# Taking the warm-up matmuls off TensorE in an attention and feed-forward kernel

## Chip, cores and metric

The kernel runs on one core of a Trainium2 chip. The metric is the device time of one execution in microseconds (us). The kernel before takes 144.61 us (median of 3 runs, 144.1 to 144.9).

## What is computed

The reference is a transformer block in float32 over x of 8 batches x 256 tokens x 128 features: single-head attention on the layer-normalised input, layer norm and residual, then a four-layer feed-forward with ternary weights and per-output scales, layer norm and residual.

```python
def attn(x, W_qkv):                       # W_qkv: 384 x 128
    q, k, v = split(einsum('bnd,ed->bne', x, W_qkv))
    a = softmax(einsum('bnd,bmd->bnm', q * 128 ** -0.5, k))
    return einsum('bnm,bmd->bnd', a, v)

def ffn(x):                               # 128 -> 512 -> 512 -> 512 -> 128
    h = silu((x @ w1.T) * s1) * ((x @ w2.T) * s2)
    h = gelu((h @ h1.T) * sh1)
    h = gelu((h @ h2.T) * sh2)
    return (h @ w3.T) * s3

x = x + layernorm(attn(layernorm(x), W_qkv))
x = x + layernorm(ffn(layernorm(x)))
```

## The kernel before

The 16 tiles of 128 tokens go through the kernel in five blocks of 2, 4, 4, 4 and 2 tiles. Each engine has one instruction stream, written out by hand; an instruction that needs another engine's result waits on a semaphore at its place in the stream, and all that stands behind it on its engine waits too. So the order of calls at the end of each engine's function is the schedule.

The stages of block b, by the names of the functions on TensorE: x_transposes(b) transposes the normalised input (matmuls against the identity `ident`, line 941); g_projection(b) multiplies it with the product of the query and key weights, which qk_product computes once from `wa_raw` (line 1121); v_projection(b) gives the values; scores(b, g) the scores of batch g of the block; probs_transposes(b, g) transposes the exponentials (line 992); attend(b, g) multiplies them with the values; attention_transposes(b) turns the result back (line 1017); x2_transposes(b) transposes the layer-normed sum (line 1024); up(b, o) computes both up-projections of hidden slice o (lines 1049, 1052); begin and end of A1, A2 and A3 are the layers h1, h2 and w3 (lines 1085, 1091); y_transposes(b) turns the block's output back (line 1112). Products of float32 data are made of high and low parts of type f32r: in the attention part each product is three matmuls (high x high, high x low, low x high), all issued in `product` (line 916).

Between the stages the other engines work. ScalarE copies the high part of each PSUM tile (xT_high, gT_high, v_high, pT_high, x2T_high, all through line 281), splits the weights (w12_high, h1_high, line 371), sums the low halves of the weights (low_sum, line 393) and computes exp, silu and gelu. VectorE writes the low parts (line 578), the row maxima neg_max (line 623), the layer-norm statistics and the normalised rows xn (line 595). GpSimd sets constants at the start (lines 226 to 231, `ident` among them) and computes the reciprocal roots (line 236). SyncE issues the loads in one order: x of block 0, the attention weights, x of block 1, w12, the scales, h1, x of block 2, h2, and so on.

keep_warm(bank, n) issues n matmuls of 128 x 128 weights with 256 columns of bf16, all read from the tile `warm` of zeros that GpSimd sets in its first own instruction (line 226). Their results land in a PSUM bank that holds nothing needed then, and nobody reads them. TensorE waits for `warm` before its first group. The groups and their places are in the order at the end of the TensorE function: 10 at the very start, 12 after qk_product, 8 after x_transposes(0), 1 ahead of g_projection(1), 3 ahead of scores(1, 0), 2 ahead of probs_transposes(1, 0) and 12 ahead of probs_transposes(1, 1); 48 in all.

Of the kernel before, what the change touches and what calls it, by code (L numbers as in the profile page):

```python
# [7 lines left out]
P = 128  # L8
# [17 lines left out]
def width(b):  # L26
    return SIZES[b] * P


def tiles(b):  # L30
    return slice(T0[b], T0[b + 1])
# [10 lines left out]
def sandwich_kernel(nc, x, w_attn, w12, h1, h2, w3, scales, out):  # L42
# [9 lines left out]
    with ctx:  # L52
        def sb(name, shape, dt=f32):
            return ctx.enter_context(nc.sbuf_tensor(name, shape, dt))

        def bank(name):
            return ctx.enter_context(nc.psum_tensor(name, [P, 512], f32))

        def sem(name):
            return ctx.enter_context(nc.semaphore(name))  # L60
# [13 lines left out]
        ident = sb("ident", [P, P])  # L74
        minus_half = sb("minus_half", [P, TB])
        ones = sb("ones", [P, 1])
        warm = sb("warm", [P, 512], mybir.dt.bfloat16)
        low_bits = sb("low_bits", [P, KT * HID])
        low_sums = sb("low_sums", [P, 4])
        flags = sb("flags", [1, 4])  # L80
# [36 lines left out]
        F = [bank(f"F{i}") for i in range(4)]  # L117
        A = [bank(f"A{i}") for i in range(4)]
# [26 lines left out]
        x_loaded = [sem(f"x_loaded{b}") for b in range(BLOCKS)]  # L145
        wa_loaded, w12_loaded, sc_loaded = sem("wa_loaded"), sem("w12_loaded"), sem("sc_loaded")
        h1_loaded, h2_loaded, w3_loaded = sem("h1_loaded"), sem("h2_loaded"), sem("w3_loaded")
        warm_ready = sem("warm_ready")
        zeroed, ident_ready = sem("zeroed"), sem("ident_ready")
        qk_summed, qk_copied, qk_split, qk_ready = sem("qk_summed"), sem("qk_copied"), sem("qk_split"), sem("qk_ready")  # L150
        wv_split, wv_ready = sem("wv_split"), sem("wv_ready")
# [39 lines left out]
        @block.sync  # L191
        def _(sp):
            def load_x(b):
                sp.dma_start(xs[:, tiles(b), :].rearrange("p (g j) d -> p g (j d)", j=2),
                             x_view[:, G0[b]:G0[b + 1], :]).then_inc(x_loaded[b], 16)

            def store(b):
                if b == LAST:
                    sp.wait_ge(last_ready, 1)
                else:  # L200
                    sp.wait_ge(out_ready, b + 1)
                sp.dma_start(out_view[:, G0[b]:G0[b + 1], :],
                             outs[:, tiles(b), :].rearrange("p (g j) d -> p g (j d)", j=2)).then_inc(out_stored, 16)

            load_x(0)
            sp.dma_start(wa_raw[:, :], w_attn).then_inc(wa_loaded, 16)
            load_x(1)
            sp.dma_start(w12_raw[:, :], w12).then_inc(w12_loaded, 16)
            sp.dma_start(sc[:, :], scales).then_inc(sc_loaded, 16)
            sp.dma_start(h1_raw[:, :, :], h1.rearrange("(k p) o -> p k o", p=P)).then_inc(h1_loaded, 16)  # L210
            load_x(2)
            sp.dma_start(h2_raw[:, :, :], h2.rearrange("(k p) o -> p k o", p=P)).then_inc(h2_loaded, 16)
            load_x(3)
            load_x(4)
            sp.dma_start(w3_raw[:, :], w3).then_inc(w3_loaded, 16)
            store(0)
            store(1)
            store(2)
            store(3)
            store(4)  # L220
            sp.wait_ge(out_stored, 16 * BLOCKS)


        @block.gpsimd
        def _(pool):
            nc.gpsimd.memset(warm[:, :], 0.0).then_inc(warm_ready, 1)  # L226
            nc.gpsimd.memset(ident[:, :], 0.0).then_inc(zeroed, 1)
            nc.gpsimd.memset(minus_half[:, :], -0.5).then_inc(zeroed, 1)
            nc.gpsimd.memset(ones[:, :], 1.0).then_inc(zeroed, 1)
            pool.wait_ge(zeroed, 3)  # L230
            nc.gpsimd.affine_select(out=ident[:, :], in_=ident[:, :], compare_op=ALU.not_equal, fill=1.0, base=0,
                                    pattern=[[-1, P]], channel_multiplier=1).then_inc(ident_ready, 1)

            def rsqrt(ln, b):
                pool.wait_ge(var_ready[ln], b + 1)
                nc.gpsimd.tensor_tensor(rstd[:, ln, tiles(b)], ve[:, ln, tiles(b)], minus_half[:, 0:SIZES[b]],  # L236
                                        ALU.pow).then_inc(rstd_ready[ln], 1)

            def lo_part(n, b, o):
                c = slice(0, width(b))  # L240
                pool.wait_ge(a_hi_ready[n], KT * b + o + 1)
                pool.wait_ge(a_full[n], KT * b + o + 1)
                nc.gpsimd.tensor_tensor(a_lo[n][:, o, c], act_full[:, o, c], a_hi[n][:, o, c].bitcast(f32),
                                        ALU.subtract).then_inc(a_lo_pool[n], 1)

            def last_add(b):
                pool.wait_ge(yn_ready, T0[b + 1])
                pool.wait_ge(x1_ready, b + 1)
                nc.gpsimd.tensor_tensor(outs[:, tiles(b), :], y_n[:, 0:SIZES[b], :], x1[:, tiles(b), :], ALU.add).then_inc(out_ready, 1)

            rsqrt(LN_X, 0)
            rsqrt(LN_X, 1)
            rsqrt(LN_X, 2)
            rsqrt(LN_O, 0)
            rsqrt(LN_X1, 0)
            rsqrt(LN_O, 1)
            rsqrt(LN_X1, 1)
            rsqrt(LN_X, 3)
            rsqrt(LN_X, 4)
            rsqrt(LN_Y, 0)  # L260
            rsqrt(LN_O, 2)
            rsqrt(LN_X1, 2)
            rsqrt(LN_Y, 1)
            rsqrt(LN_O, 3)
            last_add(0)
            last_add(1)
            rsqrt(LN_X1, 3)
            rsqrt(LN_Y, 2)
            rsqrt(LN_O, 4)
            last_add(2)  # L270
            rsqrt(LN_X1, 4)
            rsqrt(LN_Y, 3)
            last_add(3)
            rsqrt(LN_Y, 4)
# [636 lines left out]
        def _(pe):  # L911
# [18 lines left out]
            def read_flag(n):  # L930
                pe.wait_ge(flags_ready, (1, 1, 2, 2)[n])
                flag[n] = pe.value_load(flags[0:1, n:n + 1].bitcast(mybir.dt.int32))

            def x_transposes(b):
                if b > 1:
                    pe.wait_ge(gT_ready, b)
                    if SIZES[b - 1] == 4:
                        pe.wait_ge(pT_ready, G0[b])
                for t in range(SIZES[b]):
                    pe.wait_ge(xn_ready, T0[b] + t + 1)  # L940
                    last = nc.tensor.transpose(lane(b).xT_bank[:, t * P:(t + 1) * P], lane(b).xn[:, t, :], ident[:, :])
                last.then_inc(xT_in_psum, 1)

            def g_projection(b):
                c = slice(0, width(b))
                pe.wait_ge(xT_ready, b + 1)
                if b == 0:
                    pe.wait_ge(qk_ready, 1)
                product(lane(b).gT_bank[:, c], [(qk_hi[:, :], qk_lo[:, :], lane(b).xT[0][:, c], lane(b).xT[1][:, c])]).then_inc(gT_in_psum, 1)
# [16 lines left out]
            def scores(b, g):  # L966
                s = lane(b).s_bank[g]
                (x_hi, x_lo), (g_hi, g_lo) = lane(b).xT, lane(b).gT
                pe.wait_ge(gT_ready, b + 1)
                if b > 1 and g == 0:  # L970
                    pe.wait_ge(x2T_ready, b)
                if b > 1 and g == 1:
                    pe.wait_ge(oT_ready, b)
                keys = slice(g * SEQ, (g + 1) * SEQ)
                for j in range(2):
                    c = slice((2 * g + j) * P, (2 * g + j + 1) * P)
                    last = product(s[:, j * SEQ:(j + 1) * SEQ], [(g_hi[:, c], g_lo[:, c], x_hi[:, keys], x_lo[:, keys])])
                last.then_inc(scores_ready, 1)
# [133 lines left out]
                    last = nc.tensor.transpose(A[2][:, t * P:(t + 1) * P], yT[:, t * P:(t + 1) * P], ident[:, :])  # L1112
                last.then_inc(y_in_psum, 1)

            def keep_warm(bank, n):
                for _ in range(n):
                    nc.tensor.matmul(bank[:, 0:256], warm[:, 0:P], warm[:, 0:256], start=True, stop=True)  # L1117

            def qk_product():
                pe.wait_ge(wa_loaded, 16)  # L1120
                nc.tensor.matmul(F[3][:, 0:D], wa_raw[:, 0:D], wa_raw[:, D:2 * D], start=True, stop=True).then_inc(qk_summed, 1)

            pe.wait_ge(warm_ready, 1)
            keep_warm(A[0], 10)
            qk_product()
            pe.wait_ge(ident_ready, 1)
            keep_warm(A[0], 12)
            x_transposes(0)
            keep_warm(A[0], 8)
            g_projection(0)  # L1130
            x_transposes(1)
            v_projection(0)
            scores(0, 0)
            keep_warm(F[0], 1)
            g_projection(1)
            v_projection(1)
            probs_transposes(0, 0)
            keep_warm(F[3], 3)
            scores(1, 0)
            attend(0, 0)  # L1140
            scores(1, 1)
            attention_transposes(0)
            sum_flags(0)
            keep_warm(F[3], 2)
            probs_transposes(1, 0)
            read_flag(W12)
            read_flag(H1)
            keep_warm(F[3], 12)
            probs_transposes(1, 1)
            x2_transposes(0)  # L1150
            attend(1, 0)
# [136 lines left out]
```

## Time and profile before

| | |
|---|---|
| median of 3 runs | 144.61 us |
| the profiled execution | 144.72 us |
| its span, first to last instruction | 142.9 us |
| TensorE matmul busy | 127.7 us (89%), 749 matmuls |
| VectorE busy | 112.7 us (79%) |
| ScalarE busy | 113.3 us (79%) |
| GpSimd busy | 24.7 us (17%) |
| warm-up matmuls busy (30 into A, 18 into F) | 6.1 and 2.6 us |
| mean granted TensorE clock over the span | 0.991 |

The profiled execution is 1.8 us longer than its span. Busy time of TensorE is that of pipelined matmuls: the duration of one matmul contains its way through the array, so that the distance between two starts, not the duration, says how fast the engine takes them. PE is TensorE's matmuls, PEld its weight loads, ACT ScalarE, DVE VectorE, POOL GpSimd. A line such as L916 is the line of the kernel that issued the instruction; several stages share a helper's line, so they are told apart by their place in time and by their tiles. The tiles of block 0 borrow a part of act_full, a_hi and a_lo, so `act_full` or `a_hi` in an attention row of the first 20 us is block 0. The granted clock is 1.00 for TensorE at 2.4 GHz and 0.50 at 1.2 GHz.

### The profile page before, as it was taken

The numbers are of one execution on the slowest core, as the hardware profiler recorded it, in microseconds if no ns is written. First come the engines' busy times: TensorE is split into PE (matmuls) and PEld (weight loads), VectorE is DVE, ScalarE is ACT, GpSimd is POOL, SyncE is SP. The second block draws the span as 40 slices with busy tenths as digits, with TensorE's granted clock in tenths as the row PEclk, the third lists the DMA queues.
The fourth block names the chain that finished last, engine by engine and source line by source line (L and its number), as shares of the span: only waits on it lengthen the run. The fifth ranks groups of instructions, "written<-read, shape, count | busy, mean of one in ns | idle before, by whom it ended". The sixth has DMA issues, their size and how long they took to land.

```text
span 142.9 us, 2559 instructions
## 1 busy us (share of the span) xinstructions
PE 127.7 (89%) x749; PEld 106.7 (75%) x749; DVE 112.7 (79%) x362; ACT 113.3 (79%) x218; POOL 24.7 (17%) x33
## 2 busy tenths in 40 slices
PE   6987977999978999999999999999799999799930
PEld 3766855899975888888868888877578888589820
DVE  1766898999958998998889968958997597597553
ACT  3176998999999874949859996999964999968930
POOL 3400211002500000702000025510002052002301
PEclk9999999999999999999999999999999999999996
DMA  4999000000000000000000000120000002000021
GB/s 125 277 367 366 24 7 0 0 5 2 0 5 0 0 0 7 0 5 0 0 0 0 5 2 0 41 76 0 0 0 5 0 5 73 0 0 7 0 76 37
DMA packets 3857, 5.41 MB, mean 38 GB/s; under 512 B 384, under 2 KB 2560, under 8 KB 3840
## 3 DMA queue, kind: packets, MB, share of 16 engines
q1 hardware_dynamic: 3840, 5.19, 11.1%
q8 instruction: 10, 0.16, 0.4%
q14 instruction: 7, 0.06, 0.1%
HBM read 4.14 MB, written 1.05 MB: 36 GB/s over the span
## 4 chain that ended last, share of the span: by engine, by line
PE 53%; ACT 18%; issue 10%; DVE 8%; DMA 5%; POOL 2%; SPq 2%; POOLq 1%; DVEq 0%; ACTq 0%
PE F L1085 16%; PE F L1091 16%; PE A L916 8%; DMA h_raw<-h 5%; PE F L1049 4%; PE F L1052 3%; ACT a_hi L351 3%; ACT act_full L343 3%; ACT h_hi L371 2%; DVE act_full L666 2%; ACT silu L335 2%; DVE a_lo L578 1%; PE A L992 1%; DVE stats L582 1%; ACT probs L289 1%
## 5 line engine op out<-in xcount | busy, mean ns | idle before, releaser
L578 DVE TENSOR_TENSOR a_lo<-act_full,a_hi 128x512 fp32r<-128x512 f32 (+1 forms) x60 | 34.3, 595 | 6.6 <-ACT act_full L343 5.8
L236 POOL TENSOR_TENSOR rstd<-ve,minus_half 128x4 f32<-128x4 f32 (+1 forms) x20 | 18.9, 949 | 109.5 <-DVE ve L589 89.6
L1085 PE MATMUL F<-a_hi,h_hi 128*128 128x512 f32 (+1 forms) x160 | 37.4, 355 | 0.2 <-DVE act_full L666 0.2
L1091 PE MATMUL F<-a_lo,h_hi 128*128 128x512 f32 (+1 forms) x160 | 36.5, 350 | 0.0
L1091 PEld LDWEIGHTS F<-a_lo,h_hi 128*128 128x128 f32 x160 | 26.8, 189 | 4.2
L1085 PEld LDWEIGHTS F<-a_hi,h_hi 128*128 128x128 f32 x160 | 25.9, 189 | 4.0 <-DVE act_full L666 0.4
L351 ACT ACTIVATE a_hi<-F,sc 128x512 fp32r<-128x512 f32 (+1 forms) x40 | 24.2, 629 | 5.6 <-PE F L1091 5.4
L343 ACT ACTIVATE act_full<-F,sc 128x512 f32<-128x512 f32 (+1 forms) x40 | 24.3, 638 | 0.0
L666 DVE SCALAR_TENSOR_TENSOR act_full<-F,sc,silu 128x512 f32<-128x512 f32 (+1 forms) x20 | 12.5, 640 | 2.4 <-ACT silu L335 2.1
L335 ACT ACTIVATE silu<-F,sc 128x512 f32<-128x512 f32 (+1 forms) x20 | 11.5, 602 | 3.4 <-PE F L1052 3.3
L1049 PE MATMUL F<-x2T_hi,w_hi 128*128 128x512 f32 (+1 forms) x40 | 11.4, 367 | 1.7 <-DVE act_full L666 1.1
L1052 PE MATMUL F<-x2T_lo,w_hi 128*128 128x512 f32 (+1 forms) x40 | 10.9, 353 | 0.0
L1049 PEld LDWEIGHTS F<-x2T_hi,w_hi 128*128 128x128 f32 x40 | 6.3, 189 | 3.9 <-issue 2.3
L582 DVE BATCH_NORM_STATS2 stats<-A 128x6 f32<-128x128 f32 x30 | 6.8, 285 | 1.7 <-PE A L1112 1.5
L335 ACT ACT_TABLE_LOAD x6 | 7.7, 1283 | 0.1
L1052 PEld LDWEIGHTS F<-x2T_lo,w_hi 128*128 128x128 f32 x40 | 7.0, 189 | 1.1
L1117 PE MATMUL A<-warm 128*128 128x256 bf16 x30 | 6.1, 381 | 1.3 <-POOL warm L226 1.3
L585 DVE BATCH_NORM_AGGREGATE mv<-stats 128x2 f32<-128x6 f32 x64 | 6.5, 159 | 0.7
L1091 PE MATMUL A<-a_lo,w_hi 128*128 128x512 f32 (+1 forms) x20 | 5.8, 364 | 1.4 <-DVE a_lo L578 1.4
L674 DVE CAST a_hi<-act_full 128x512 fp32r<-128x512 f32 (+1 forms) x20 | 6.9, 367 | 0.1
L289 ACT ACTIVATE probs<-A,neg_max 128x256 f32<-128x256 f32 x14 | 6.5, 476 | 0.0
L351 ACT ACT_TABLE_LOAD x5 | 6.4, 1283 | 0.1
(137 smaller groups left out, 235.4 us busy)
## 6 DMA issues: line engine op xcount, KB each, us to landing
h_raw<-h SPq DMA_DIRECT2D x2, 1024.0 KB, 8.9
xs<-x SPq DMA_DIRECT2D x3, 256.0 KB, 7.9
out<-outs SPq DMA_DIRECT2D x3, 256.0 KB, 2.1
w_raw<-w SPq DMA_DIRECT2D x1, 512.0 KB, 4.9
xs<-x SPq DMA_DIRECT2D x2, 128.0 KB, 5.9
w_raw<-w SPq DMA_DIRECT2D x1, 256.0 KB, 9.2
out<-outs SPq DMA_DIRECT2D x2, 128.0 KB, 1.7
wa_raw<-w_attn SPq DMA_DIRECT2D x1, 192.0 KB, 2.4
```

The lines of the kernel that those rows point to most:

```text
L236: nc.gpsimd.tensor_tensor(rstd[:, ln, tiles(b)], ve[:, ln, tiles(b)], minus_half[:, 0:SIZES[b]], ALU.pow).then_inc(rstd_ready[ln], 1)
L335: nc.scalar.activation(silu1[:, o % 2, c], F[2 * (o % 2)][:, c], ACT.Silu, scale=sc[:, S_W1 + o:S_W1 + o + 1]).then_inc(silu_ready, 1)
L343: nc.scalar.activation(act_full[:, o, c], F[o][:, c], ACT.Gelu, scale=sc[:, s:s + 1]).then_inc(a_full[n], 1)
L351: nc.scalar.activation(a_hi[n][:, o, c], F[o][:, c], ACT.Gelu, scale=sc[:, s:s + 1]).then_inc(a_hi_ready[n], 1)
L578: nc.vector.tensor_tensor(dst, full, hi.bitcast(f32), ALU.subtract).then_inc(done, 1)
L582: last = nc.vector.bn_stats(stats[:, ln, T0[b] + t, :], tile(t))
L666: nc.vector.scalar_tensor_tensor(act_full[:, o, c], F[2 * (o % 2) + 1][:, c], sc[:, S_W2 + o:S_W2 + o + 1], silu1[:, o % 2, c], ALU.mult, ...
L916: last = nc.tensor.matmul(out, w, v, start=(n == 0 and m == 0), stop=(n == len(terms) - 1 and m == 2))
L1049: nc.tensor.matmul(bank, w_hi, x_hi, start=True, stop=False)
L1052: last = nc.tensor.matmul(bank, w_hi, x_lo, start=False, stop=True)
L1085: nc.tensor.matmul(out, terms[k][0], terms[k][2], start=(k == 0), stop=False)
L1091: last = [nc.tensor.matmul(out, terms[k][0], terms[k][3], start=False, stop=(k == KT - 1)) for out, terms in groups]
```

## The change

The seven calls of keep_warm, the function, the wait for `warm`, the memset on GpSimd, the semaphore and the tile are taken out. The order of all else on every engine stays.

```diff
-        warm = sb("warm", [P, 512], mybir.dt.bfloat16)
...
-        warm_ready = sem("warm_ready")
...
-            nc.gpsimd.memset(warm[:, :], 0.0).then_inc(warm_ready, 1)
...
-            def keep_warm(bank, n):
-                for _ in range(n):
-                    nc.tensor.matmul(bank[:, 0:256], warm[:, 0:P], warm[:, 0:256], start=True, stop=True)
-
...
-            pe.wait_ge(warm_ready, 1)
-            keep_warm(A[0], 10)
             qk_product()
             pe.wait_ge(ident_ready, 1)
-            keep_warm(A[0], 12)
             x_transposes(0)
-            keep_warm(A[0], 8)
             g_projection(0)
             x_transposes(1)
             v_projection(0)
             scores(0, 0)
-            keep_warm(F[0], 1)
             g_projection(1)
             v_projection(1)
             probs_transposes(0, 0)
-            keep_warm(F[3], 3)
             scores(1, 0)
             attend(0, 0)
             scores(1, 1)
             attention_transposes(0)
             sum_flags(0)
-            keep_warm(F[3], 2)
             probs_transposes(1, 0)
             read_flag(W12)
             read_flag(H1)
-            keep_warm(F[3], 12)
             probs_transposes(1, 1)
```

## Rows read from the trace of the kernel before

**Rows 1.** The page, part 4: the ended-last chain's shares of the span, by engine.

```profile
PE 53%; ACT 18%; issue 10%; DVE 8%; DMA 5%; POOL 2%; SPq 2%; POOLq 1%; DVEq 0%; ACTq 0%
```

**Rows 2.** That chain in order of time: start us, us, what.

```profile
12.70 2.25 PE A L916 x15
...
23.50 0.50 PE F L1024 x2
...
28.65 0.48 ACT silu L335
```

**Rows 3.** TensorE's timeline: start us, us (all matmuls of the row), line, tiles, count.

```profile
1.31 2.32 PE L1117 MATMUL A<-warm 128*128 128x256 bf16 x10 [1.31 <-POOL warm L226]
3.62 0.80 PE L1121 MATMUL F<-wa_raw 128*128 128x128 f32 x2
4.21 2.77 PE L1117 MATMUL A<-warm 128*128 128x256 bf16 x12
6.77 0.61 PE L941 MATMUL F<-ident,act_full 128*128 128x128 f32 x2
7.19 1.06 PE L1117 MATMUL A<-warm 128*128 128x256 bf16 x8
8.84 0.39 PE L916 MATMUL F<-a_hi,qk_hi 128*128 128x256 f32 x1 [0.59 <-DVE a_lo L578]
...
13.04 0.40 PE L916 MATMUL A<-xT_lo,qk_hi 128*128 128x512 f32 x1
13.27 0.39 PE L916 MATMUL A<-xT_hi,qk_lo 128*128 128x512 f32 x1
...
14.79 0.62 PE L992 MATMUL F<-ident,act_full 128*128 128x128 f32 x4
...
18.37 0.38 PE L1017 MATMUL F<-ident,act_full 128*128 128x128 f32 x2
...
19.21 0.65 PE L992 MATMUL A<-ident,probs 128*128 128x128 f32 x4
...
22.50 0.66 PE L992 MATMUL A<-ident,probs 128*128 128x128 f32 x4 [0.25 <-ACT probs L289]
...
24.38 0.35 PE L916 MATMUL A<-pT_hi,v_hi 128*128 128x256 f32 x1 [0.39 <-issue]
```

**Rows 4.** Timelines of ScalarE and VectorE in the same stretch.

```profile
7.96 0.37 ACT L281 ACTIVATE a_hi<-F 128x256 fp32r<-128x256 f32 x1
...
13.28 0.47 ACT L289 ACTIVATE act_full<-F,neg_max 128x256 f32<-128x256 f32 x1 [1.08 <-DVE neg_max L623]
...
15.45 0.60 ACT L281 ACTIVATE a_hi<-F 128x512 fp32r<-128x512 f32 x1
...
24.03 0.39 ACT L281 ACTIVATE x2T_hi<-F 128x256 fp32r<-128x256 f32 x1 [0.49 <-PE F L1024]
...
12.56 0.68 DVE L623 TENSOR_REDUCE neg_max<-F 128x2 f32<-128x512 f32 x1
...
16.08 0.69 DVE L578 TENSOR_TENSOR a_lo<-F,a_hi 128x512 fp32r<-128x512 f32 x1 [0.23 <-ACT a_hi L281]
```

**Rows 5.** Busy time by stretches: us, busy per engine (instructions), granted clock, DMA, GB/s.

```profile
1.30:7.20 5.90, 5.89 (x27) 4.11 (x28) 3.40 (x20) 1.20 (x3) 2.24 (x6) 1.00 0.89 246
40.00:44.00 4.00, 2.85 (x18) 2.27 (x18) 2.80 (x7) 3.97 (x11) 0.00 (x0) 1.00 0.00 0
136.30:138.40 2.10, 1.19 (x5) 0.68 (x5) 0.62 (x3) 0.59 (x2) 0.00 (x0) 1.00 0.14 47
138.40:140.30 1.90, 0.00 (x0) 0.00 (x0) 1.52 (x8) 0.00 (x0) 0.71 (x1) 1.00 0.00 0
140.30:142.90 2.60, 0.00 (x0) 0.00 (x0) 0.47 (x2) 0.00 (x0) 0.00 (x0) 0.51 0.15 50
```

**Rows 6.** The tile warm: instruction, output, count, duration ns min/median/max, first and last start.

```profile
L1117 PE MATMUL A<-warm x30: 272/421/421, 1.3 to 8.0; 128*128 128x256 bf16 x30
...
L1117 PE MATMUL F<-warm x18: 269/272/283, 11.4 to 22.0; 128*128 128x256 bf16 x18
```

## Prediction

> **What bounds the kernel now.** I read these views in this order. First the shares of the chain that ended last: it lies on TensorE for 53% of the span, on ScalarE for 18%, on VectorE for 8% [rows 1]. Second the same chain in order of time. Its early part follows the loads; then it rests on TensorE for 2.25 us from 12.70 (g_projection(1), v_projection(1)), after that mostly on VectorE and GpSimd up to x2_transposes(0) at 23.50, on TensorE from there to 28.65, where ScalarE takes over with silu [rows 2], and the rest of it alternates between these two, mostly TensorE. No piece of the chain carries line 1117, the warm-up matmuls. Third, TensorE's own timeline of the first 28 us [rows 3], which shows what each warm-up group stands between. Last the rows of ScalarE and VectorE that the first steps wait for [rows 4] and the granted clock [rows 5].
>
> **TensorE's clock in this trace.** The same warm-up matmul takes a median of 421 ns in its first 30 places and 272 ns in its last 18 [rows 6]. The twelve after qk_product take 6.77 - 4.21 = 2.56 us, 0.213 us each, which is 256 columns at 1.2 GHz; the eight from 7.19 take 1.06 us with the last one's full length, so about 0.11 each, which is 2.4 GHz [rows 3]. So the engine ran at the low level from its first matmul at 1.31 to about 7.2 us. (The granted clock in the row of 1.3 to 7.2 reads 1.00; the durations speak against it there, and I go by them.) It had then been at work 5.9 us, of which the last 3.6, from 3.62, without a hole. It stayed at the high level through 40 to 44 us, with 2.85 us of matmuls in 4.0. From 140.3 on it read 0.51: ahead of that lie 2.1 us with 1.19 us of matmuls and 1.9 us with none [rows 5].
>
> **The change part by part: the work itself.** 48 matmuls (30 of a median of 421 ns and 18 of 272 ns [rows 6]), their 48 weight loads and one memset on GpSimd go. Each group covers a wait of TensorE, so I cost their removal at nothing:
> - The 12 ahead of x_transposes(0) end at 6.77, with the transposes right behind, so these may start earlier. ScalarE hides it: it comes to the copy of xT only at 7.96, as w12_high stands ahead of it [rows 3, 4].
> - The 8 after it and the one before g_projection(1) end well before 8.84 and 12.70, where VectorE's low parts release TensorE [rows 3].
> - The 3 before scores(1, 0) take 3 x 0.11 = 0.3 us; attend(0, 0), which follows, waits for the low part that VectorE has written at 16.08 + 0.69 = 16.77 [rows 4].
> - The 2 before probs_transposes(1, 0) take 0.2 us and are no piece of the chain; the 12 before probs_transposes(1, 1) are done before it, as it starts at 22.50 after 0.25 us of idle time that ScalarE's probabilities end [rows 3].
> - The memset stood ahead of the identity on GpSimd. The first reader of the identity is at 6.77, and the memset is done before 1.31; the cover is over 5 us [rows 3].
>
> **The early clock.** Without the warm-up TensorE has, before 8.84, only qk_product at 3.62 and two transposes near 6.4. From 8.84 it works without large holes: g_projection(0), four transposes, v_projection(0), scores(0, 0). At the low level I double the spacing seen at the high one: 0.23 us for a 512-column step (13.04 to 13.27), 0.11 for 128 columns (the twelve of v_projection(1), 14.79 - 13.50 = 1.29), and for 256 I take 0.12, between these; so 0.46, 0.22 and 0.24 at the low level. The two transposes from 6.77 to 7.19 support it with 0.21 each [rows 3]. Then: g_projection(0) to 9.6, four transposes to 10.4, six steps of v_projection(0) to 11.8, six of scores(0, 0) to 13.2. neg_max, 0.68 us, moves from 12.56 to 13.4 and the exponentials from 13.28 to 14.1 [rows 4]. g_projection(1) runs 13.2 to 14.5 instead of 12.70 to 13.5 [rows 3]; the twelve steps of v_projection(1) follow. When the clock rises decides the rest. Before, it took 5.9 us from the first matmul; from 8.84 this gives 14.7. The ends: the 3.6 us without a hole give 12.4, and 5.9 us from the end of the transposes gives 16.3. With 14.7 eleven of the twelve steps run at 0.11, to 15.95 instead of 14.79: probs_transposes(0, 0) is 1.15 us late. With 12.4 it is 0.3 to 0.4 late (by the exponentials), with 16.3 about 2.0. ScalarE's copy at 15.45 waits for these transposes, and from there to 23.5 the two other engines have hardly a hole: ScalarE's only one is 0.49 us at 24.03, and that wait is for the late chain itself [rows 4]. So the delay passes on in full. I take 1.15, ends 0.4 and 2.0.
>
> **The late clock.** Between scores(1, 1), which ends about 18.4, and attend(1, 0) at 24.38 TensorE's own work is only 0.38 + 0.65 + 0.66 + 0.50 = 2.19 us of transposes and two tiny flag sums, in 6.0 us; the 14 warm-up matmuls were the rest [rows 3]. The rows have no such stretch in mid-kernel: what the engine did in it lies between what it did before the fall at the end and what it did from 40 to 44, and is the more like the first, as short spells of transposes stand among pauses, the longest 22.50 - 19.86 = 2.6 us [rows 3, 5]. So I take a fall. Work then resumes at 24.38 + 1.15 = 25.5 at the low level, where TensorE is on the chain up to 28.6 [rows 2]. With 3.6 us until the clock is back half of that is lost, 1.8, less some 0.3 us of small holes that TensorE has there: 1.5 us. The ends: 0.5, if the fall comes so late that the clock is back after a third of that; and 3.0, half of 5.9, if it needs 5.9 us again [rows 2, 3]. After 28.6 nothing catches it up, as ScalarE and then TensorE carry the chain without a pause [rows 2].
>
> A rule of the Trainium skill bears on this place (TensorE: Matmul & The Clock Gate, Part 4: PE-mode transpose): it says that a transpose does not count as TensorE activity for the clock gate as a matmul does. No row here isolates that; with it the stretch would be nearly idle for the gate and the same 1.5 us would be more certain, without it only less so.
>
> **Sum.** 144.72 (the profiled execution, its span of 142.9 and 1.8 around it) + 0 + 1.15 + 1.5 = 147.4. The median of the runs is 0.11 below the profiled execution, so I forecast 147.3 for the median.
>
> **The rivals.**
> - Only the early loss. The high level, once reached, lasts through 18.4 to 24.4, as it lasted 1.9 us with no matmul at all at the end (138.4 to 140.3) [rows 5]. Time: 144.6 + 0.7 to 2.0, centre 145.8. The trace speaks for it in that TensorE never rests longer than about 2.6 us at one go here (19.9 to 22.5). The Trainium skill (same page, Part 1: The HAM clock gate (the "warmup" mystery)) says that for modelling the ramp costs less than 1% of a typical kernel's span; 1% of 142.9 would be 1.4 us, so a time up to 146.0, a result of this rival's kind. It is a rule on one ramp; whether there are two is what the trace leaves open.
> - The clock does not rise until the dense work after 25 us. Before, the 2.32 us of warm-up from 1.31 did not raise it, and the projections and scores come in spells that wait for the other engines [rows 3]. Then v_projection(1) ends at 17.2, the transposes at 18.0 (2.75 late), scores(1, 0), attend(0, 0) and scores(1, 1) take 1.4 each and put attention_transposes(0) at 22.3 instead of 18.37, 3.9 late; with 1.5 to 3.0 at 24 to 28 the time is 150.0 to 151.5, or 149 if it rises on the way.
> - No loss that can be measured: the clock rises by 12.4 and holds. 144.9 to 145.2.
> - Faster. If the clock rises about as early as before (by 10 us) and holds, the warm-up groups could have been paid for: up to 0.3 ahead of x_transposes(0), 0.3 ahead of scores(1, 0), 0.2 ahead of probs_transposes(1, 0), together 0.8, so 143.8. Against it: line 1117 is nowhere on the chain [rows 2], and each group ends before another engine's release.
>
> **How the numbers follow.** Forecast (both losses) 0.42; early loss alone 0.26; late rise 0.13; no loss 0.13; faster 0.06. About 0.5% (0.7 us) is what a measurement of this kernel can tell from no change. Slower by more: 0.42 + 0.26 + 0.13 = 0.81; within it: 0.13; faster: 0.06. The range runs from the lower end of no loss to just short of the late rise's 150.0, taking in its cheaper part: 144.9 to 149.9. It leaves out the faster case and some 0.10 of the late rise, 0.16 in all.
>
> **What would show it.** In the trace of after: matmuls of g_projection(0), v_projection(0) and scores(0, 0) 0.21 to 0.24 us apart, and a granted clock that turns to the high level between 12.4 and 16.3; probs_transposes(0, 0) starting near 16 instead of 14.79; a second low stretch from somewhere in 22 to 25.5 to about 29, with up(0, *) twice as far apart; from 32 us on the same pattern as before, shifted by some 2.65 us. It would be wrong if the granted clock stays high in 19 to 25 (then 145.8), or if ScalarE's copy of 15.45 comes on time though TensorE was slow (then the cover I took as absent is there), or if some other work than line 1117 starts earlier and stays earlier.

## The result, and the profile after

The changed kernel takes 147.38 us (median of 4 runs, 146.74 to 147.88) against 144.71 before: a ratio of 1.0186, 95% interval 1.0148 to 1.0225. It is slower by 1.9%, where 147.3 was forecast. A second set of runs, shown below, gave 1.012 (1.0048 to 1.0191); all nine runs of the changed kernel have a median of 146.98. Medians here are over all runs of a kernel, while the ratios leave out the runs that lie more than 1.5% above the fastest of their kernel.

The head of the page of after, its busy times and its granted clock in 40 slices:

```profile
span 146.0 us, 2463 instructions
PE 123.6 (85%) x701; PEld 105.0 (72%) x701; DVE 112.8 (77%) x362; ACT 113.4 (78%) x218; POOL 24.3 (17%) x32
...
PEclk9999999599999999999999999999999999999995
```

TensorE has 48 matmuls less and is busy 4.1 us less, and yet the span is 3.1 us longer (142.9 before). The granted clock has a dip in the eighth slice of 40, about 26 to 29 us, that before did not have.

TensorE's timeline of after (the stages' lines are three less than before: L913 is L916, L989 is L992; qk_product's L1114 was L1121), answering to [rows 3]:

```profile
4.46 0.80 PE L1114 MATMUL F<-wa_raw 128*128 128x128 f32 x2 [4.46 <-DMA wa_raw<-w_attn]
...
9.47 0.58 PE L913 MATMUL F<-a_hi,qk_hi 128*128 128x256 f32 x1 [1.44 <-DVE a_lo L575]
...
14.12 0.63 PE L913 MATMUL A<-xT_lo,qk_hi 128*128 128x512 f32 x1
14.55 0.63 PE L913 MATMUL A<-xT_hi,qk_lo 128*128 128x512 f32 x1
...
15.51 0.41 PE L913 MATMUL A<-wv_hi,xT_hi 128*128 128x128 f32 x1
15.72 0.34 PE L913 MATMUL A<-wv_lo,xT_hi 128*128 128x128 f32 x1
15.89 0.27 PE L913 MATMUL A<-wv_hi,xT_lo 128*128 128x128 f32 x1
16.00 0.28 PE L913 MATMUL A<-wv_hi,xT_hi 128*128 128x128 f32 x1
...
16.68 0.62 PE L989 MATMUL F<-ident,act_full 128*128 128x128 f32 x4
...
24.39 0.66 PE L989 MATMUL A<-ident,probs 128*128 128x128 f32 x4 [2.63 <-ACT probs L286]
...
26.28 0.55 PE L913 MATMUL A<-pT_hi,v_hi 128*128 128x256 f32 x1 [0.39 <-issue]
26.63 0.41 PE L913 MATMUL A<-pT_lo,v_hi 128*128 128x256 f32 x1
...
30.00 0.29 PE L913 MATMUL A<-pT_hi,v_lo 128*128 128x256 f32 x1
```

The 512-column steps are 0.43 us apart at 14.1 (0.23 in [rows 3]), the 128-column steps 0.21 apart up to 15.72 and 0.11 from 15.89. So the high level came at about 15.8 us instead of 7.2. From 26.28 a 256-column matmul takes 0.41 us again; at 30.00 it takes 0.29.

Busy time by stretches, after, answering to [rows 5] (the same columns):

```profile
22.00:24.00 2.00, 0.00 (x0) 0.00 (x0) 1.78 (x10) 2.00 (x6) 0.43 (x1) 1.00 0.02 4
24.00:26.00 2.00, 1.15 (x6) 0.69 (x6) 1.78 (x6) 1.51 (x6) 0.70 (x1) 1.00 0.00 0
26.00:28.00 2.00, 1.72 (x8) 1.75 (x9) 1.77 (x6) 1.98 (x3) 0.00 (x0) 0.52 0.00 0
28.00:30.00 2.00, 2.00 (x13) 1.74 (x12) 1.03 (x4) 0.93 (x3) 0.00 (x0) 0.63 0.03 8
```

A clock of 0.52 over 2 us that begin at the high level is a fall at about 26.1; 0.63 in the next two is 1.5 us more at 0.50, so it was back at 29.5. Ahead of the fall TensorE rested for 2.63 us at one go. The fall did not come in that rest but 1.7 us after work had begun again at 24.39.

ScalarE's timeline of after, answering to [rows 4]:

```profile
11.45 0.63 ACT L368 ACTIVATE h_hi<-h_raw 128x512 fp32r<-128x512 f32 x1 [0.54 <-DMA h_raw<-h]
...
17.34 0.60 ACT L278 ACTIVATE a_hi<-F 128x512 fp32r<-128x512 f32 x1 [0.65 <-PE F L989]
...
28.79 0.47 ACT L332 ACTIVATE silu<-F,sc 128x256 f32<-128x256 f32 x1 [0.69 <-PE F L1049]
29.64 0.48 ACT L332 ACTIVATE silu<-F,sc 128x256 f32<-128x256 f32 x1 [0.38 <-PE F L1049]
```

Two marks cut the span into three parts. The first is the start of ScalarE's copy of h1's first part, which waits for the load of h1: 11.45 here, and before it was this row:

```profile
10.80 0.63 ACT L371 ACTIVATE h_hi<-h_raw 128x512 fp32r<-128x512 f32 x1 [0.92 <-DMA h_raw<-h]
```

The second is the copy of the transposed probabilities: 17.34 here, 15.45 in [rows 4]. Up to the first mark it is the loads, as long as this copy waits for its load; between the two lies the early clock; behind the second the late one. The 3.1 us are then 0.65 of the loads, (17.34 - 11.45) - (15.45 - 10.80) = 1.24 of the early clock, and (146.0 - 17.34) - (142.9 - 15.45) = 1.21 of the late one. The first term stands in no step of the prediction. ScalarE's new waits on TensorE (0.65 at 17.34, 0.69 and 0.38 ahead of the silus) show that TensorE is the late one in the other two. Nearly all of the 3.1 us is there by 34 us, as the same loading of ScalarE's function table in the two traces shows, before first:

```profile
30.67 1.28 ACT L351 ACT_TABLE_LOAD   x1
```

```profile
33.66 1.28 ACT L348 ACT_TABLE_LOAD   x1
```

It is 2.99 us later, and all that follows adds 0.1.

### The profile page after: what moved, and what is told of

Same layout as the page of the kernel before. It is cut to its first block, busy times and chain, and to the rows that moved or that the text cites. A ratio compares the mean times of both kernels' runs of the same rounds, so it can differ in the third digit from the quotient of the medians.

```text
span 146.0 us, 2463 instructions
## 1 busy us (share of the span) xinstructions
PE 123.6 (85%) x701; PEld 105.0 (72%) x701; DVE 112.8 (77%) x362; ACT 113.4 (78%) x218; POOL 24.3 (17%) x32
## 4 chain that ended last, share of the span: by engine, by line
PE 56%; ACT 18%; issue 9%; DVE 7%; DMA 4%; POOL 2%; SPq 1%; POOLq 1%; DVEq 0%; ACTq 0%
PE F L1082 16%; PE F L1088 16%; PE A L913 9%; PE F L1046 4%; DMA w_raw<-w 4%; PE F L1049 3%; ACT a_hi L348 3%; ACT act_full L340 3%; PE F L913 2%; ACT silu L332 2%; DVE act_full L663 2%; ACT h_hi L368 2%; PE A L989 1%; DVE a_lo L575 1%; DVE stats L579 1%
## 5 line engine op out<-in xcount | busy, mean ns | idle before, releaser
L1046 PEld LDWEIGHTS F<-x2T_hi,w_hi 128*128 128x128 f32 x40 | 6.8, 203 | 3.8 <-issue 2.2
L989 PE MATMUL A<-ident,probs 128*128 128x128 f32 x28 | 4.3, 280 | 3.6 <-ACT probs L286 3.6
L579 DVE BATCH_NORM_STATS2 stats<-xs 128x6 f32<-128x128 f32 x16 | 3.6, 280 | 4.5 <-DMA xs<-x 4.5
L989 PEld LDWEIGHTS A<-ident,probs 128*128 128x128 f32 x28 | 3.1, 140 | 4.8 <-ACT probs L286 4.6
```

The lines of the kernel that those rows point to most:

```text
L579: last = nc.vector.bn_stats(stats[:, ln, T0[b] + t, :], tile(t))
L1046: nc.tensor.matmul(bank, w_hi, x_hi, start=True, stop=False)
```

## The experiments

Eight experiments on six kernels, in two sets; each set shares its runs of before (medians 144.83 and 144.82). Each has one trace.

**The changed kernel again.** No edit.

> The changed kernel once more, unaltered, for a second trace and more runs. In its first trace the loads landed some 0.65 us later than before (w12 read at 7.63 instead of 7.00, the copy of h1 at 11.45 instead of 10.80), which no step of the prediction contains. Theory (the loads vary from run to run and the change has no part in it): h1's copy on ScalarE starts anywhere in 10.8 to 11.5, and the span follows it; span 145.0 to 146.0. Rival (the idle TensorE, or the missing memset, makes the loads late): h1's copy at 11.4 or later again. Both: low level to 12.4 to 16.3 us, and a second low stretch between 22 and 30 us. Time 146.7 to 147.9.

146.8 us, ratio 1.012 (1.0048 to 1.0191), span 145.1.

```profile
10.73 0.63 ACT L368 ACTIVATE h_hi<-h_raw 128x512 fp32r<-128x512 f32 x1 [0.39 <-DMA h_raw<-h]
...
16.55 0.60 ACT L278 ACTIVATE a_hi<-F 128x512 fp32r<-128x512 f32 x1 [0.43 <-PE F L989]
```

ScalarE's timeline has h1's copy at 10.73, earlier than before's 10.80. So the change does not make the loads late every time, and the 0.65 us in the first trace need no cause in it. That it has no part at all in the loads is not shown: in the four traces without the early groups in which h1's copy waited for its load it started at 10.73 to 11.45, in the four with early groups, or with transposes in their place, at 10.61 to 11.15. The two clock terms came back: 1.17 between the marks and 1.1 behind them. The second low stretch:

```profile
24.00:26.00 2.00, 1.27 (x7) 0.84 (x6) 1.70 (x5) 1.51 (x5) 0.07 (x1) 0.76 0.00 0
...
28.00:30.00 2.00, 2.00 (x16) 1.83 (x16) 1.23 (x4) 1.68 (x4) 0.00 (x0) 0.89 0.00 0
```

The same reckoning as above gives a fall at 25.0 and a rise at 28.4, with 0.50 in between.

**The early groups alone.**

```diff
-            keep_warm(F[0], 1)
...
-            keep_warm(F[3], 3)
...
-            keep_warm(F[3], 2)
...
-            keep_warm(F[3], 12)
```

> Warm-up groups 10, 12 and 8 (up to g_projection(0)) kept, the groups 1, 3, 2 and 12 taken out. Theory (two separate losses): the clock rises near 7 us as before, the copy of probs_transposes(0, 0) stays at 15.4 to 15.5, the granted clock falls between 22 and 26 us and is back by 29 to 31; the late loss alone, 1.1 to 1.5 us: 145.8 to 146.2. Rival (there is one loss, the early one, and the late fall only hits a kernel that is late already): 144.7.

146.25 us, ratio 1.009 (1.0048 to 1.0131), span 144.3. TensorE and, below, the stretches:

```profile
22.85 0.66 PE L992 MATMUL A<-ident,probs 128*128 128x128 f32 x4 [2.63 <-ACT probs L289]
...
24.74 0.55 PE L916 MATMUL A<-pT_hi,v_hi 128*128 128x256 f32 x1 [0.39 <-issue]
```

```profile
24.00:26.00 2.00, 1.61 (x8) 1.43 (x8) 1.77 (x5) 1.60 (x3) 0.00 (x0) 0.64 0.03 8
26.00:28.00 2.00, 2.00 (x11) 1.78 (x11) 1.25 (x5) 1.03 (x2) 0.00 (x0) 0.50 0.00 0
28.00:30.00 2.00, 2.00 (x18) 1.96 (x18) 1.63 (x7) 1.86 (x4) 0.00 (x0) 1.00 0.00 0
```

The clock rose early (the copy came 4.66 us after that of h1; before 4.65) and fell at about 24.6 all the same, behind the same rest of 2.63 us. It was back at 28.0, earlier than expected. The late loss therefore exists by itself. It cost 1.0 us behind the second mark and 1.4 by the medians. The record has the mean granted clock of every run, which only falls can lower (one comes at the end of every trace), since the low level at the start reads 1.00. All ten runs lie at 0.976 or below, where 37 of the 44 runs of before lie at 0.982 or above. The traced run has 0.976 and two others 0.974; six have 0.963 to 0.969. A low stretch of twice the length would lower the mean by 3.4 x 0.5 / 144.3 = 0.012, so these six may have had the longer one that a later trace shows; that is an estimate, as they have no trace.

**The late groups alone**, ten runs and, later, one more.

```diff
-            keep_warm(A[0], 10)
...
-            keep_warm(A[0], 12)
...
-            keep_warm(A[0], 8)
...
-            keep_warm(F[0], 1)
...
-            keep_warm(F[3], 3)
```

> Only the groups of 2 and 12 ahead of probs_transposes(1, 0) and (1, 1) kept; 10, 12, 8, 1 and 3 taken out. Theory (two separate losses): low level to about 12.4 to 16.3 us, the copy of probs_transposes(0, 0) 0.4 to 2.0 us late, no fall between 22 and 30 us; the early loss alone, 1.2 to 1.9 us: 145.8 to 146.6. Rival (late matmuls hold the clock only where it had been up for long): a fall in spite of them, 146.7 to 147.9 as with the whole change.

> The kernel with the late groups alone, one look more, for the same question: after a rise at 13.0 to 13.5 the copy of the transposed probabilities starts about 4.9 us after the copy of h1, after a rise at 15 to 16 about 5.9 by the theory that the moment of the rise sets the early loss; 4.9 in any case by the rival that the loss hangs on the missing matmuls of the late groups. No fall in 20 to 30 us by both. Span 143.2 to 144.6.

145.39 us, ratio 1.0045 (1.001 to 1.008), and 145.02 in the single run; spans 143.4 and 143.2. In neither trace did the clock fall between 20 and 30 us, and no run of the ten has a mean clock under 0.985. The rise is to be seen in TensorE's timelines, first that of the ten runs, then that of the single one:

```profile
13.04 0.53 PE L916 MATMUL A<-xT_hi,qk_hi 128*128 128x512 f32 x1
13.41 0.40 PE L916 MATMUL A<-xT_lo,qk_hi 128*128 128x512 f32 x1
13.65 0.40 PE L916 MATMUL A<-xT_hi,qk_lo 128*128 128x512 f32 x1
```

```profile
12.08 0.41 PE L916 MATMUL F<-a_hi,a_lo 128*128 128x256 f32 x1
12.29 0.35 PE L916 MATMUL F<-a_hi 128*128 128x256 f32 x1
12.47 0.28 PE L916 MATMUL F<-a_lo,a_hi 128*128 128x256 f32 x1
```

The high level came near 13.3 and near 12.4 us, and the time between the marks was 4.89 and 4.65, a loss of 0.24 and 0. That is less than expected: the early loss is not a constant. The loss of 0 came about because h1 set the pace there: its copy, VectorE's low part of xT behind it (12.17 against 11.95) and g_projection(1) (12.92 against 12.70) were all 0.22 us later than before, and so was the copy of the transposed probabilities. TensorE had caught up by then. That the loss hangs on the moment of the rise is the likely reading, and the next trace was taken for it.

**The changed kernel a third time**, one run, for that moment.

> The changed kernel a third time, one look, for the moment at which the clock rises. Theory (the moment differs from run to run and sets the early loss): with a rise at 13.0 to 13.5 the copy of the transposed probabilities starts about 4.9 us after the copy of h1 (4.65 before), with a rise at 15 to 16 about 5.9. Rival (the early loss does not hang on the clock): 5.8 to 5.9 whatever the rise. Span 144.5 to 146.0.

```profile
9.85 0.58 PE L913 MATMUL F<-a_hi,qk_hi 128*128 128x256 f32 x1 [1.61 <-DVE a_lo L575]
...
14.07 0.56 PE L913 MATMUL A<-xT_hi,qk_hi 128*128 128x512 f32 x1
14.48 0.39 PE L913 MATMUL A<-xT_lo,qk_hi 128*128 128x512 f32 x1
```

148.44 us, span 146.6, longer than the 144.5 to 146.0 expected. The rise was near 14.3, between the two cases of the expectation, and the time between the marks 5.77, which by itself would fit the rival. But in this run w12 landed late (read at 8.01), so g_projection(0) started only at 9.85; and h1's copy at 11.18 waited for no load, as the copy ahead of it had waited for TensorE, so the first mark does not show the loads here. What should count is how long TensorE works on at the low level from g_projection(0). In that measure, chosen after the run, the five executions without the early groups line up: 3.7, 4.5, 4.5, 6.0 and 6.3 us from g_projection(0) to the rise, and 6.96, 7.09, 7.10, 7.64 and 7.87 us from it to the copy of the transposed probabilities (before 6.61). That is 0.35 to 1.26 us over before, and 0.5 for this run. The pair at 4.5 is this run and one with the late groups, which speaks against a part of the late groups in it. A measure chosen afterwards on five traces supports the theory and does not prove it. The late stretch was longer too:

```profile
24.00:26.00 2.00, 1.40 (x7) 0.90 (x7) 1.59 (x5) 1.31 (x4) 0.50 (x1) 0.67 0.00 0
26.00:28.00 2.00, 2.00 (x10) 2.00 (x11) 1.79 (x5) 1.88 (x3) 0.00 (x0) 0.50 0.00 0
28.00:30.00 2.00, 2.00 (x11) 1.74 (x11) 1.05 (x4) 1.20 (x3) 0.00 (x0) 0.50 0.03 8
30.00:32.00 2.00, 2.00 (x13) 2.00 (x13) 1.39 (x6) 1.11 (x3) 0.00 (x0) 0.62 0.00 0
```

From 24.7 to 31.5 it was low, 6.8 us instead of 3.4, and the part behind the second mark lost 2.2 us instead of 1.2. So the late loss has at least two sizes.

**Transposes as the late filler.** The early groups stay, 1, 3 and 2 are out, and instead of the last 12:

```diff
-            keep_warm(F[3], 12)
+            for _ in range(12):
+                nc.tensor.transpose(F[3][:, 0:P], ident[:, :], ident[:, :])
```

> As with the early groups alone (10, 12, 8 kept, 1, 3 and 2 out), but at the place of the last 12 warm-up matmuls stand 12 transposes of the identity into the same bank, about as long (0.11 us each against 0.12). Theory (any work of TensorE holds the clock): no fall between 22 and 30 us, 144.6 to 144.9. Rival (a transpose does not count for the clock as a matmul does, as the Trainium skill says in TensorE: Matmul & The Clock Gate, Part 4): the clock falls between 22 and 26 us as without any filler, 145.8 to 146.2.

145.02 us, ratio 1.0016 (0.9974 to 1.0059), span 142.5; the granted clock stayed:

```profile
20.30 1.50 PE L1146 MATMUL F<-ident 128*128 128x128 f32 x12 [0.92 <-DVE flags L714]
22.01 0.66 PE L992 MATMUL A<-ident,probs 128*128 128x128 f32 x4 [0.21 <-ACT probs L289]
...
24.09 0.28 PE L916 MATMUL A<-pT_lo,v_hi 128*128 128x256 f32 x1
```

The early groups alone, from which it differs by these 12 transposes, took 146.25. In the trace the transposes did what the matmuls do, and the rival, which has the clock fall as without any filler, falls. Whether they hold it as surely is open: four of the ten runs (145.92 to 147.23 us) have a mean granted clock of 0.967 to 0.978, as against 7 of 44 runs of before at 0.978 or below, all seven at 146.0 us or more. None of these has a trace, so it is not shown whether the clock fell in mid-kernel in them, in some runs of before too, or only earlier at the end.

**Transposes as the early filler.** The late groups stay as before; fill_with_transposes(bank, n) issues n transposes as in the last experiment.

```diff
-            keep_warm(A[0], 10)
+            pe.wait_ge(ident_ready, 1)
+            fill_with_transposes(A[0], 7)
             qk_product()
             pe.wait_ge(ident_ready, 1)
-            keep_warm(A[0], 12)
+            fill_with_transposes(A[0], 12)
             x_transposes(0)
-            keep_warm(A[0], 8)
+            fill_with_transposes(A[0], 8)
```

> As before, but the three early groups are transposes of the identity instead of matmuls of the tile warm: 7, 12 and 8 of them, each 0.21 us apart at the low level like the matmuls they replace; the late groups are the matmuls of before. Theory (transposes count for the clock like matmuls, as the run with late transposes suggests): the clock rises by 8 to 9 us, 144.6 to 145.1. Rival (transposes hold a high level but do not raise a low one): the clock rises only between 12.4 and 16.3 us, as with the late groups alone, 145.2 to 146.0.

144.59 us, ratio 0.9988 (0.9956 to 1.002), span 142.8.

```profile
2.16 1.73 PE L1121 MATMUL A<-ident 128*128 128x128 f32 x7 [2.16 <-POOL ident L231]
...
4.27 2.69 PE L1121 MATMUL A<-ident 128*128 128x128 f32 x12
6.80 0.38 PE L941 MATMUL F<-ident,act_full 128*128 128x128 f32 x2
7.02 1.04 PE L1121 MATMUL A<-ident 128*128 128x128 f32 x8
```

Twelve in 6.80 - 4.27 = 2.53 us are 0.21 each, the two of x_transposes(0) 0.11 each: the high level came at about 6.8, after nothing but transposes and qk_product. So they raise the clock as well as hold it.

**The lean version**, with 12, 8 and the last 12.

```diff
-            keep_warm(A[0], 10)
...
-            keep_warm(F[0], 1)
...
-            keep_warm(F[3], 3)
...
-            keep_warm(F[3], 2)
```

> Only the groups of 12 (after qk_product), 8 (after x_transposes(0)) and 12 (ahead of probs_transposes(1, 1)) kept; 10, 1, 3 and 2 out. Theory (a warm-up group is worth something only if it brings the high level before about 9 us or bridges the pause at 20 to 24 us): the clock rises between 7.2 and 10 us, no fall, 144.6 to 145.0, no difference from before. Rival (the first ten are needed, since without them the engine has been at work for only 5 us by 9): rise at 10.5 or later and 0.2 to 1.2 us lost, 145.0 to 146.0.

144.8 us, ratio 1.001 (0.9972 to 1.0048), span 142.6.

```profile
3.78 0.76 PE L1121 MATMUL F<-wa_raw 128*128 128x128 f32 x2 [3.78 <-DMA wa_raw<-w_attn]
4.34 2.77 PE L1117 MATMUL A<-warm 128*128 128x256 bf16 x12
6.90 0.62 PE L941 MATMUL F<-ident,act_full 128*128 128x128 f32 x2
7.32 1.07 PE L1117 MATMUL A<-warm 128*128 128x256 bf16 x8
```

The high level came at 7.3 though TensorE had first worked at 3.78; the copy of the transposed probabilities came 4.64 us after that of h1. So sixteen of the 48 warm-up matmuls were of no use that can be measured. None of the variants is faster than before beyond its interval, so no version that beats both kernels is in sight here.

## Why the prediction was right, step by step

- **The removal costs nothing, and gives nothing.** Right as far as it was tested: in lean the groups of 10, 1, 3 and 2 go and the time stays, 1.001 of before. The faster rival (143.8) did not show. The cost of the work of the other three groups by itself was not measured, as the clock changes with them.
- **The early clock, 1.15 us, ends 0.4 and 2.0.** The low-level spacings were right (0.43 for 512 columns against 0.46 taken, 0.21 for 128 and 256 against 0.22 and 0.24). The rise lay in the range of 12.4 to 16.3 in all five executions in which no early group ran (15.8, 14.9, 14.3, 13.3, 12.4). The whole change lost 1.24 and 1.17 between the marks in its first two traces, close to the value taken. The third lost 1.12 there, but from g_projection(0) on only 0.5, and the rest came with w12's late landing. The kernel with the late groups alone lost 0.24 and 0, and 0.6 by its median. So 1.15 is one case of something that varies with the moment, and the lower end should have been 0. The 3.6 us behind the end at 12.4 stand on a weak reading: by [rows 5] TensorE was busy 5.89 of 5.90 us from 1.31, so what sets the last 3.6 apart is only one distance of 0.41 between two starts (3.21 and 3.62) where the others are 0.21. It was in part luck that the figure served; lean supports it, as its clock rose 3.5 us after its first matmul.
- **It passes on in full.** Right: with the late groups in place the part behind the second mark is 127.5 us (143.4 - 15.92, 143.2 - 15.67) against 127.45 before. Nothing catches up and nothing more is lost.
- **The late clock, 1.5 us, ends 0.5 and 3.0.** The fall and its cause, the thin work of TensorE in that stretch, were right: it came in all three traces of the changed kernel and with the early groups alone, and in none of the six traces where matmuls or transposes filled the pause. The size was 1.2, 1.1, 2.2 and 1.0 us, in the range of 0.5 to 3.0. The term mis-sized is the time at the low level that meets TensorE's work: I took 3.6 us, in the first trace it was 26.28 to 29.5, 3.2, less the small holes.
- **The sum.** 144.72 + 1.15 + 1.5 against 144.72 + 1.24 + 1.21 + 0.65 in the first trace. That the median of the first four runs fell on the forecast owes something to luck, namely to late loads, at least in the profiled one of them; the second trace, with loads as before, had 2.2 us in all, and 147.3 is some 0.3 us above the median of all nine runs.
- **The rivals.** The early loss alone is refuted by the falls. The rise only after 25 us did not occur. No loss at all is outside the interval of the whole change (1.0048 at least), though one trace with the late groups shows no early loss. A 6.8 us low stretch in the third trace is the nearest to it and gave 148.4.
- **The two rules of the Trainium skill.** By TensorE: Matmul & The Clock Gate, Part 1: The HAM clock gate (the "warmup" mystery), the ramp costs less than 1% of a typical span. The early ramp alone agrees: 0.45% with the late groups in place, and 1.24 us, 0.9%, in the first trace; the whole change, 1.2 to 1.9%, does not, because this kernel pays a second time in mid-kernel. By its Part 4: PE-mode transpose, a transpose does not count for the gate as a matmul does; here 12 float32 transposes held the high level and 19 with qk_product raised it, so the measurement decides against it, for the float32 transposes that nc.tensor.transpose issues here. The profile lists them as matmuls and does not say in which mode the array ran them.

## What to carry to other kernels

A warm-up is to be judged by where TensorE's next work on the chain lies: it is worth up to the work that would otherwise run there at half speed, and a stretch in mid-kernel with little work for TensorE (here 2.2 us in 6.0) can need one as much as the start. Compare the distance between equal matmuls at several places before believing the granted clock of the first microseconds. Since the moment of rise and fall moves from run to run, the loss is a spread and not a number, and a gain or loss of 1% needs several traces to be explained, as it did here.

## What the runs showed of the hardware

- Before the first change of level the granted clock reads 1.00 while matmuls run at 0.21 us per 256 columns; the rows are wrong there (up to 7.2 us in before, up to 15.8 in after).
- The low stretch in mid-kernel was 3.4 us long in three traces and 6.8 in one; three of the four, both lengths among them, are of the same kernel. In all four the longest rest ahead of it was 2.63 us, and the fall came 0.7 to 1.7 us after TensorE had begun to work again.
- Float32 transposes through the array (0.11 us each at the high level, 0.21 at the low one) both raised and held the clock in the one trace of each kind.
- The landing of the same loads differs from run to run, and the span moves with it. The first reader of w12 waited for its load in all ten traces and started at 6.77 to 8.01 us; h1's copy waited for its load in eight and started at 10.61 to 11.45. That is as large as the effects looked for; cutting the span at h1's copy takes it out where the copy waited for its load.
